# Cross attention's rows: one fp32 product made into three products of rounded halves

## The reference

```python
def _L0_xattn_ref(teacher_logits, teacher_features, Wq, bq, Wk, bk):
    query = einsum('bnc,dc->bnd', teacher_features, Wq) + bq
    key = einsum('bnc,dc->bnd', teacher_features, Wk) + bk
    energy = einsum('bnd,bmd->bnm', query, key)
    attention = softmax(energy, axis=-1)
    x_m = einsum('bln,bmn->blm', teacher_logits, attention)

x = _layernorm(x + _L0_attn_ref(x, ...))
x = _layernorm(x + _L0_xattn_ref(x, ctx_1024, ...))
x = _layernorm(x + _L0_ffn_ref(x, ...))
```

## Time and profile before

| | us |
|---|---|
| median of 3 runs | 395.31 (394.3 to 395.33) |
| profiled execution, its time | 396.07 |
| profiled execution, its span | 394.3 |
| TensorE busy | 382.7 (97%) |
| VectorE busy | 279.7 (71%) |
| ScalarE busy | 264.4 (67%) |
| GpSimd busy | 197.6 (50%) |

### The profile page before, as it was taken

How to read it: one execution, slowest core, us unless ns; L and a number is a source line. 1 busy time by engine, 2 the same in 40 slices (tenths; PEclk the granted TensorE clock), 3 DMA queues, 4 the chain that set the end, 5 groups by cost and what they waited for, 6 DMA issues and landing times.

```text
span 394.3 us, 8310 instructions
## 1 busy us (share of the span) xinstructions
PE 382.7 (97%) x2528; PEld 343.9 (87%) x2528; DVE 279.7 (71%) x781; ACT 264.4 (67%) x660; POOL 197.6 (50%) x334
## 2 busy tenths in 40 slices
PE   6889999999999999999999999999999999999995
PEld 4767899989999989999989978888889998989995
DVE  2888998868878778878768866765858546644445
ACT  3689997777687777687768684765765643534343
POOL 1399775654776744677546655787856100000000
PEclk9999999999999999999999999999999999999999
DMA  7530600000000000000000495232222212343311
GB/s 256 191 118 17 233 23 7 2 0 2 0 30 0 0 0 0 0 0 0 0 0 1 124 362 182 91 105 81 81 80 95 70 65 79 100 138 103 92 62 53
DMA packets 16709, 28.04 MB, mean 71 GB/s; under 512 B 2198, under 2 KB 7816, under 8 KB 16680
## 3 DMA queue, kind: packets, MB, share of 16 engines
q1 hardware_dynamic: 16536, 27.56, 21.2%
q10 hardware_dynamic: 144, 0.13, 0.1%
HBM read 26.57 MB, written 1.11 MB: 70 GB/s over the span
## 4 chain that ended last, share of the span: by engine, by line
PE 88%; DVE 4%; ACT 2%; POOL 2%; issue 2%; DMA 1%; SPq 0%; DVEq 0%; ACTq 0%; POOLq 0%
PE bank L687 24%; PE bank L688 23%; PE bank L689 23%; PE bank L830 6%; PE bank L840 5%; PE bank L829 3%; PE bank L789 2%; DMA stage<-in_pieces 1%; PE bank L783 1%; PE bank L797 1%; POOL queryT L1545 1%; DVE by_sin L1317 1%; DVE wk_lo L1187 0%; PE bank L803 0%; DVE wq_lo L1187 0%
## 5 line engine op out<-in xcount | busy, mean ns | idle before, releaser
L984 ACT ACTIVATE hid<-bank,small_sb 128x512 f32<-128x512 f32 x48 | 33.0, 687 | 56.2 <-PE bank L689 47.5
L1204 DVE TENSOR_TENSOR hid<-hid,gate_rows 128x512 f32<-128x512 f32 (+1 forms) x44 | 31.9, 724 | 48.4 <-ACT hid L984 48.2
L688 PE MATMUL bank<-w_lo,hid_hi 128*128 128x256 f32 (+1 forms) x200 | 56.3, 282 | 0.0
L1545 POOL TENSOR_TENSOR queryT<-by_cos,by_sin 128x512 f32<-128x512 f32 x32 | 43.1, 1347 | 22.7 <-DVE by_sin L1317 21.9
L1553 POOL TENSOR_SCALAR nprobs<-probs,rsums 128x128 f32<-128x128 f32 x64 | 25.7, 402 | 44.2 <-DVE rsums L1333 30.6
L687 PE MATMUL bank<-xT_hi,wq_hi 128*128 128x256 f32 x128 | 38.8, 303 | 2.4 <-DVE wq_lo L1187 1.2
L1187 DVE TENSOR_TENSOR hid_lo<-hid,hid_hi 128x512 fp32r<-128x512 f32 x48 | 36.1, 752 | 5.4 <-ACT hid_hi L1005 5.4
L689 PE MATMUL bank<-x2T_hi,w_lo 128*128 128x512 f32 (+1 forms) x100 | 39.6, 396 | 0.0
L688 PEld LDWEIGHTS bank<-w_lo,hid_hi 128*128 128x128 f32 (+1 forms) x200 | 37.7, 188 | 2.1
L830 PE MATMUL bank<-keyT,queryT 128*128 128x256 f32 x128 | 38.2, 380 | 0.0
L1056 ACT COPY swapped<-bank 64x512 f32<-64x512 f32 x40 | 23.3, 583 | 22.1 <-PE bank L689 21.6
(11 more groups left out here) (162 smaller groups left out, 1238.6 us busy)
## 6 DMA issues: line engine op xcount, KB each, us to landing
stage<-in_pieces SPq DMA_DIRECT2D x8, 512.0 KB, 4.6
w_raw<-in_w SPq DMA_DIRECT2D x4, 1024.0 KB, 12.8
gate_rows<-gates_d SPq DMA_DIRECT2D x16, 256.0 KB, 3.1
gate_rows<-gates_d SPq DMA_DIRECT2D x8, 224.0 KB, 3.1
w_raw<-in_w SPq DMA_DIRECT2D x2, 768.0 KB, 7.9
gate_rows<-gates_d SPq DMA_DIRECT2D x8, 192.0 KB, 2.8
gate_rows<-gates_d SPq DMA_DIRECT2D x8, 160.0 KB, 2.6
xraw<-in_xt SPq DMA_DIRECT2D x4, 256.0 KB, 2.6
```

Of the source, the lines that this page charges most:

```text
L688: nc.tensor.matmul(o, sh, ml, start=False, stop=False, **kw)
L984: nc.scalar.activation(hid[:, u % 2, :], z_bank[u % 3][:], ACT.Relu, bias=b1_cols[:, i % NC:i % NC + 1]).then_inc(relu_done, 1)
L1204: nc.vector.tensor_tensor(own, own, gate_rows[rows, i % 3, :], ALU.mult).then_inc(gated, 1)
L1545: nc.gpsimd.tensor_tensor(o.rearrange("p a t -> p (a t)"), by_cos[:, r % 2, :], by_sin[:, r % 2, :], ALU.add).then_inc(rope_add, 1)
```

## The change

TensorE makes `m0` and `m1` by `three` in place of one fp32 product for each chunk. For that both turned operands are split: in slots `a` and `n` ScalarE now copies the bank to `attT` or `x1T`, which become `fp32r`, and signals `turn_hi`; VectorE then waits for `turn_hi` and writes bank less high half to `att_lo` or `x1_lo`, which lie in the part of `x2T_hi` and `x2T_lo` that the last batch fills. That memory belongs to the weights' stage before; so in batch 0 ScalarE waits for the last piece's low before slot `a`, the last piece is moved ahead of it, and TensorE waits for slot `a` before it enters the loop. The gates' scratch moves from `x1T` to `e_exp`. After the loop ScalarE gets slot `n` in the step of chunk 5.

The tables of times are changed too. What this does to the orders: on TensorE in the loop `out0 0`, `out0 1`, `out0 2`, `out0 3` go before the value products that they followed, `e` before `values0 3`, turn 9 before `a`; between `n` and `m0` nothing changes. On VectorE in the loop, `q2`, `q3`, `k1`, `e`, `v0`, `q6` change places with a neighbour or two, the addition for `m0` goes before reciprocal 9, `probs_lo` 9 before `a`. On ScalarE some neighbours change places, `probs_hi` 9 goes before `a`. On GpSimd normalisation 15 goes before rotary `q2` and `k1` before normalisation 2. Before the loop: TensorE takes score 2, `k1`, `e` and only then the second half of cross attention's projections; ScalarE takes exponential 0 before `q3`; GpSimd copies for the energies before `q2`, adds `k1` before normalisation 1, and makes both parts of `wv_lo` before normalisation 3, not around it; the piece `o0` comes later and `o3` earlier.

```diff
--- before.py
+++ after.py
@@ -74,10 +74,7 @@
 
 
 
-SLOT_AT = {"q0": -1.25, "k0": -1, "q1": -0.75, "q2": -0.5, "q3": 1.75,
-           "k1": 2.75, "q4": 4.75, "v1": 5.5, "v0": 6.5, "q5": 7.25, "q6": 7.75, "q7": 11,
-           "n": 25.5, "m0": 26.5, "m1": 26.75, "y": 29.35,
-           "e": 3.75, "a": 12}
+SLOT_AT = {"q0": -1.482, "k0": -1, "q1": -0.75, "q2": -0.088, "q3": 1.829, "k1": 2.092, "q4": 4.75, "v1": 5.5, "v0": 6.596, "q5": 7.25, "q6": 7.75, "q7": 11, "n": 25.365, "m0": 26.472, "m1": 26.7, "y": 29.35, "e": 3.635, "a": 12.152}
 WINDOW = -2.5
 
 
@@ -104,23 +101,20 @@
 
 
 WORK_AT = {
-    "pe": {"score": 0, "slot": 0, "turn": 3, "values0": 7.25, "values1": 9, "out0": 9.25,
-           "out1": 11},
-    "act": {"next x": 11.6, "slot": 0, "exp": 0.74, "probs_hi": 3, "heads_hi0": 7.25, "heads_hi1": 9.25,
-            "normed 1": 25.2, "normed 2": 28.95},
-    "dve": {"slot": 0, "top": -0.5, "recip": 0.74, "e recip": 4.4, "probs_lo": 3, "heads_lo0": 7.25, "heads_lo1": 9,
-            "residual": 22.75, "moments 1": 23, "moments 2": 26.75},
-    "pool": {"next x": 11.7, "slot": 0, "normalise": 0.5, "e copy": 1.4, "e norm": 4.9, "norm 1": 22.75, "norm 2": 26.75, "keep": 28.75},
+    "pe": {"score": -0.038, "slot": 0, "turn": 3, "values0": 7.675, "values1": 9.084, "out0": 9.03, "out1": 11},
+    "act": {"next x": 11.041, "slot": 0, "exp": 0.739, "probs_hi": 3.038, "heads_hi0": 7.25, "heads_hi1": 9.25, "normed 1": 25.2, "normed 2": 28.95},
+    "dve": {"slot": 0, "top": -0.5, "recip": 0.74, "e recip": 4.4, "probs_lo": 3, "heads_lo0": 7.25, "heads_lo1": 9, "residual": 22.75, "moments 1": 23, "moments 2": 26.75},
+    "pool": {"next x": 11.7, "slot": 0, "normalise": 0.5, "e copy": 1.371, "e norm": 4.982, "norm 1": 22.75, "norm 2": 26.75, "keep": 28.75},
 }
 
...
-
-LATER = {"act": {"y": -0.05, "e": 0.35}, "dve": {"n": -0.5, "m0": -0.75, "m1": -0.25, "y": -0.25}}
...
+
+LATER = {"act": {"y": -0.05, "e": 0.35, "q3": -0.061, "q4": -0.025, "m0": -0.261, "q0": -0.139}, "dve": {"n": -0.5, "m0": -0.75, "m1": -0.25, "y": -0.25, "q1": -0.124, "q6": 0.493, "q3": -0.588, "q2": 0.175, "q0": 0.229}}
 
 
 SOURCES = ["q0", "k", "q1", "q2", "v", "q3", "o0", "o1", "o2", "o3"]
 HALVES = {"q0a": ("q0", 0), "q0b": ("q0", 1), "ka": ("k", 0), "kb": ("k", 1)}
-PIECE_AT = {"q0a": -2.123, "ka": -2.057, "q0b": -2.0, "q1": -0.947, "kb": -0.758, "q2": 1.149, "v": 3.254, "q3": 4.603, "o0": 6.587, "o1": 8.1, "o2": 10.126, "o3": 12.792}
+PIECE_AT = {"q0a": -2.123, "ka": -2.057, "q0b": -2.0, "q1": -0.947, "kb": -0.758, "q2": 1.149, "v": 3.254, "q3": 4.603, "o0": 6.789, "o1": 8.1, "o2": 10.126, "o3": 11.6}
 PIECE_NAMES = list(PIECE_AT)
 LOADS = ["q0a", "ka", "tables", "q0b", "cross 0", "q1", "kb", "q2", "cross 1", "v", "small", "q3", "ident", "o1", "o0", "o3", "o2"]
 LOW_AT = {"v": (2.6, 2.9), "q3": (4.6, 4.8)}
@@ -337,7 +331,7 @@
 
         ident = sb("ident", [P, P])
         res = sb("res", [P, NT, C])
-        attT = sb("attT", [P, KC, T])
+        attT = sb("attT", [P, KC, T], F32R)
         xqT = sb("xqT", [P, N])
         xkT = sb("xkT", [P, N])
         xq_now = sb("xq_now", [P, T])
@@ -346,7 +340,7 @@
         e_sum = sb("e_sum", [P, TT])
         e_rsum = sb("e_rsum", [P, TT])
         xln = sb("xln", [P, TT, C])
-        x1T = sb("x1T", [P, KC, T])
+        x1T = sb("x1T", [P, KC, T], F32R)
         moments = sb("moments", [P, TT, 2])
         bn = sb("bn", [P, TT, 6])
         var_eps = sb("var_eps", [P, TT])
@@ -369,10 +363,10 @@
         SC = NR + 4
         choice = sb("choice", [P, HT, SC])
 
-        def over_x1T(at, n):
-            return x1T[:].rearrange("p k t -> p (k t)")[:, at:at + HT * n].rearrange("p (t r) -> p t r", t=HT)
-        sig, chosen = over_x1T(0, NR), over_x1T(64, NR)
-        taken, best = over_x1T(128, SC), over_x1T(128 + HT * SC, 8)
+        def over_e_exp(at, n):
+            return e_exp[:].rearrange("p k t -> p (k t)")[:, at:at + HT * n].rearrange("p (t r) -> p t r", t=HT)
+        sig, chosen = over_e_exp(0, NR), over_e_exp(64, NR)
+        taken, best = over_e_exp(128, SC), over_e_exp(128 + HT * SC, 8)
         gate_sum = sb("gate_sum", [P, HT])
         gate_rsum = sb("gate_rsum", [P, HT])
         gates = sb("gates", [P, 2, LAST + HT * (NR + NS)])
@@ -424,6 +418,7 @@
 
         x2T_hi = sb("x2T_hi", [P, KC, N], F32R)
         x2T_lo = sb("x2T_lo", [P, KC, N], F32R)
+        att_lo, x1_lo = x2T_hi[:, :, N - T:], x2T_lo[:, :, N - T:]
         raw = ExitStack()
         w1_raw = sb("w1_raw", [P, KC, F + NR], F32, raw)
         w2_raw = sb("w2_raw", [P, NC, C], F32, raw)
@@ -452,6 +447,7 @@
 
 
         ld_ident, ld_tables, ld_res = sem("ld_ident"), sem("ld_tables"), sem("ld_res")
+        turn_hi = sem("turn_hi")
         ld_xt, x_hi_done, x_done = sem("ld_xt"), sem("x_hi_done"), sem("x_done")
         ld_stage = [sem(f"ld_stage{i}") for i in range(4)]
         ld_half = [sem(f"ld_half_{name}") for name in HALVES]
@@ -786,9 +782,9 @@
 
                     e.wait_ge(emptied, slot_count(b, "n"))
                     for k in range(KC):
-                        mm = nc.tensor.matmul(o[:, 0:C], x1T[:, k, j * P:(j + 1) * P],
-                                              attT[:, k, :],
-                                              start=k == 0, stop=k == KC - 1)
+                        rows = slice(j * P, (j + 1) * P)
+                        mm = three(o[:, 0:C], x1T[:, k, rows], x1_lo[:, k, rows], attT[:, k, :], att_lo[:, k, :],
+                                   k == 0, k == KC - 1)
                 elif kind == "e":
                     if isinstance(b, int) and b == 0:
                         after("dve", "xkT 0")
@@ -902,6 +898,7 @@
             e.wait_ge(idle_set, 1)
             keep_busy(2)
             take_turn("pe", 0, (0, "once"), doers)
+            e.wait_ge(emptied, slot_count(0, "a"))
             with e.Fori(1, B) as b:
                 take_turn("pe", b, (0, 1), doers)
 
@@ -1029,9 +1026,16 @@
 
             def slot(b, s):
                 n, kind, j = SLOTS.index(s), s[0], int(s[1:] or 0)
-                if kind in "nma":
+                if kind == "m":
                     return
                 o = proj_bank[n % 2]
+                if kind in "na":
+                    e.wait_ge(projected, slot_count(b, s))
+                    if kind == "a" and isinstance(b, int) and b == 0:
+                        piece_low(e, PIECE_NAMES[-1])
+                    nc.scalar.copy((attT if kind == "a" else x1T)[:],
+                                   o[:].rearrange("p (k t) -> p k t", k=KC)).then_inc(turn_hi, 1)
+                    return
                 if kind == "e":
                     e.wait_ge(e_topped, b + 1)
                     e.sem_inc(act_passed, 1)
@@ -1156,6 +1160,8 @@
                     split(i + 3)
                 if i == 4:
                     normed(z, 0)
+                if i == 5:
+                    slot(z, "n")
                 if i == 9:
                     normed(z, 1)
                 if i == 11:
@@ -1289,13 +1295,10 @@
                     nc.vector.tensor_reduce(e_ntop[:], o[:].rearrange("p (t s) -> p t s", t=TT),
                                             AX.X, ALU.max, negate=True).then_inc(e_topped, 1)
                     return
-                if kind == "a":
-                    e.wait_ge(projected, slot_count(b, s))
-                    nc.vector.tensor_copy(attT[:].rearrange("p k r -> p (k r)"), o[:]).then_inc(emptied, 1)
-                    return
-                if kind == "n":
-                    e.wait_ge(projected, slot_count(b, s))
-                    nc.vector.tensor_copy(x1T[:].rearrange("p k t -> p (k t)"), o[:]).then_inc(emptied, 1)
+                if kind in "na":
+                    e.wait_ge(turn_hi, 2 * b + (1 if kind == "a" else 2))
+                    hi, lo = (attT, att_lo) if kind == "a" else (x1T, x1_lo)
+                    low(lo, o[:].rearrange("p (k t) -> p k t", k=KC), hi[:]).then_inc(emptied, 1)
                     return
                 if kind == "m":
                     e.wait_ge(projected, slot_count(b, s))
```

(1 more changed line is left out.)

1 line of the change is left out of this document (added).

## The result

The kernel after the change takes 396.83 us, median of 6 runs (396.47 to 397.42); the kernel before, run beside it, 394.97 (394.3 to 395.33, 6 runs). The ratio is 1.0046, with a 95% interval of 1.0033 to 1.006: slower by 1.86 us. The profiled execution has a span of 394.7 us and a time of 396.47.

What follows compares the result with a forecast made beforehand. TensorE, busy 382.7 of 394.3 us, was taken as the bound. Terms: +2.70 for the wait, -1.42 for the products, -0.3 for the first batch, +1.0 on 395.31: forecast 396.3 us, range 394.4 to 397.9.

Steps and rivals of the forecast that it cites:

- slower by more than 0.3%: The whole kernel: measured above 396.5 us, told apart from no change; chance 0.39, beside same 0.51 and faster 0.10.
- The products: `m0` and `m1` on TensorE: 1.79 to 1.42 us, gaining 0.37 in each of three turns and 0.31 after the loop.
- The hand-over at `n`: In the loop, ScalarE's copy then VectorE's subtraction make `m0` start 0.90 us late, +2.7 us over three turns.
- bounds of 0.62 and 1.05: Delay of `m0`: at least 0.62 if ScalarE starts when VectorE did, at most 1.05 by the times at `y`.
- the choice of `y` as the nearest row: The delay at `n` sized from the like hand-over at `y`: 1.82 us where 0.98 are covered, taken as 0.90.
- Who else hides or grows it: The wait before `m0`: nobody hides it; rival of a second wait, 397.8 us, chance 0.18; rival hidden, 393.6, chance 0.10.
- No wait before `q7`: In the loop, VectorE's addition for `m0` ends at about 104.97, before `q7` at 105.17, with 0.2 us to spare.
- The hand-over at `a`: ScalarE's added copies and VectorE's subtraction at slot `a` cost zero, at most 0.5 us a turn through ScalarE's queue.
- After the loop: Three chunks of the experts cover the wait for `n`: cost zero, with 0.6 us for one late `relu` without cover.
- The reordered first batch: Work before the loop: 0.3 us gained as `wv_lo` comes earlier for `v1`; bounds 0.3 lost to 1.4 gained.
- The swaps in the loop: Reordered work in the loop's queues, such as `out0` before `values1`: zero, 0.3 us either way.

Runs made afterwards that it cites:

- fp32_products: The changed kernel with `m0` and `m1` as fp32 products of the high halves, low halves made but left out; ratio 1.0071 to the kernel before.
- no_wait: The changed kernel, but in the loop `m0` and `m1` read halves of `wk` and `m0` doesn't wait for `n`; ratio 1.0047 to the kernel before.
- m_later: The changed kernel with `m0` and `m1` behind score 11 on TensorE and their additions later on VectorE; ratio 1.0082 to the kernel before.
- order_only: The kernel before's arithmetic with the changed kernel's tables of times and its wait for slot `a` before the loop; ratio 1.0035 to the kernel before.

## Why the prediction was right, and where it was not

396.83 lies in the range of 394.4 to 397.9 and near the forecast of 396.3. But the forecast stood on 395.31 for before, and beside 394.97 the change is +1.86 us, not +1.0, and slower by more than 0.3%, which had a chance of 0.39 only. Step by step:

- **The products.** Forecast 1.79 to 1.42 us. Measured 1.42 without the 0.10 at their start, and 0.30 to 0.36 a turn by fp32_products. Right.
- **The hand-over at `n`.** That it grows by a pair in series and lands on TensorE was right. The size was 0.90, at bounds of 0.62 and 1.05; measured 0.69 (0.59 + 0.10). Mis-sized was the choice of `y` as the nearest row: there ScalarE starts 0.39 after the score product and VectorE 0.74 after ScalarE; at `n` it is 0.20 (100.93 to 101.13) and 0.62 (101.13 to 101.75), the values of the lower bound. (That bound's own terms, 0.20 + 0.59 + 0.69 + 0.04 less 0.98, make 0.54 and not 0.62; measured is 0.59.) The idle time before `m0` was forecast at 0.8 to 1.0 and is 0.45. The trace of before had the 0.20 at `n` itself, in VectorE's start. That was the nearer row, and it was kept for the bound only. 0.6 us too much over three turns.
- **Who else hides or grows it.** "No wait before `q7`" was right, and for the reason given, that the addition keeps up when `m0` is late. no_wait and m_later show how narrow this is: 0.5 and 0.9 us a turn as soon as it fails.
- **The hand-over at `a`: zero.** In the loop right. Before the loop wrong: the diff's `e.wait_ge(emptied, slot_count(0, "a"))` was named in the description and had no term in the sum. It costs 0.4, and 0.1 in the turn behind it, as the low at `a` ends too late for it.
- **After the loop.** -0.31 by the products, covered otherwise. By the rows right: from `m0`'s first product to the second one behind `m1` it was 1.96 us (265.30 to 267.26) and is 1.65 (266.11 to 267.76). The -0.26 of the whole stretch agrees, but that stretch varies by more than this from profile to profile.
- **The reordered first batch, -0.3 in bounds of +0.3 and -1.4.** This is the step that failed: it was +0.9 without the wait, outside the bounds. The prediction followed one edit, `wv_lo`, from its wait to the next one, and found the gain. It missed the same edit on `wq_lo` altogether, behind which two normalisations are late (behind the pair of `wv` TensorE waits for none), and it had no term for what the new orders do ahead of turn 0 (+0.49). The lower bound of 0.3 had no row behind it.
- **The swaps in the loop: zero, 0.3 either way.** By order_only they are +0.3 a turn with the old arithmetic, through VectorE's stretched product, and nothing on top with the new one.

So two errors of opposite sign, +0.6 and about -1.6, made the number look better than its parts: the loop was forecast at +1.6 us and was +0.9, the first batch at -0.3 and was +1.3. That 396.83 lies so near to 396.3 is luck in that part: the sign and the wait at `n` were foreseen, two thirds of the loss were not.

## What to carry to other kernels

A copy that becomes a rounding copy on one engine and a subtraction on another is 0.6 to 0.7 us longer to its reader here, and if the reader had no slack, that is paid each time, however much the products gain; so give it more cover in the same edit, and follow the bank that the reader frees, since the next slot waits for it. A reordering that starts one operation earlier by joining pieces makes what stood between the pieces late: go through the diff's tables entry by entry, engine by engine, and give every moved piece a line for what now waits behind it. A wait that is added once, ahead of a loop, needs a term too: ask when the work it names ends in that one pass. And where spans of two profiles differ by how early their loads came, compare stretches between like instructions.
